# Cross attention's output projection inside its loop over pairs of heads, and the first loads of two stages in another order

## What is computed

```
x = x + cross_attention(layernorm(x), ctx)      # 16 heads of 128, keys: 8 x 256 rows of 256
x = x + linear_attention(layernorm(x))          # 16 heads of 128, gated
x = x + mixture_of_experts(layernorm(x))        # 32 experts, top 6, and 2 shared ones

q, k = rmsnorm(x @ Wq) * gq, rmsnorm(ctx @ Wk) * gk ;  v = ctx @ Wv     # cross attention
out  = softmax(q k^T / sqrt(128)) v             # per batch and head, 64 x 256 scores
return out.reshape(512, 2048) @ Wo              # the output projection: 16 heads summed
```

## Time and profile before

| | |
|---|---|
| median of 3 executions | 1117.15 us (1112.55 to 1118.06) |
| the profiled execution, its own time | 1118.14 us |
| its span, first to last instruction | 1116.2 us |
| mean granted TensorE clock | 0.971 |
| busy: PE, PEld, DVE, ACT, POOL | 90%, 74%, 58%, 48%, 24% |
| busy in tenths over the loop of pairs, 118.7 to 355.3 us | PE 8 to 9, DVE 5, ACT 6 |

### The profile page before, as it was taken

The page is one execution under the profiler, slowest core; times in us unless marked ns, Lnnn a source line. Parts: engine busy times, 40 slices in busy tenths (PEclk is TensorE's granted clock), DMA queues, the critical chain, the costliest instruction groups (busy, mean ns, idle before and its releaser), DMA issues.

```text
span 1116.2 us, 17886 instructions
## 1 busy us (share of the span) xinstructions
PE 1008.8 (90%) x5300; PEld 829.5 (74%) x5301; DVE 649.0 (58%) x947; ACT 540.2 (48%) x888; POOL 271.5 (24%) x188
## 2 busy tenths in 40 slices
PE   6999799999998869999999998798987988898982
PEld 5787589889987648888888876676865766666761
DVE  5655355555554567777777855564555656665663
ACT  5444466666664336555555434412444545453550
POOL 2200111111111442333333224100222322232221
PEclk9999999999999979999999999999999999999897
DMA  8000622222221621221221053104498989998996
GB/s 301 1 1 1 195 71 73 70 67 74 75 85 58 170 86 57 75 69 65 73 70 62 19 181 90 38 4 146 121 294 259 306 237 315 312 297 246 320 291 153
DMA packets 107145, 151.46 MB, mean 136 GB/s; under 512 B 11888, under 2 KB 73584, under 8 KB 106992
## 3 DMA queue, kind: packets, MB, share of 16 engines
q1 hardware_dynamic: 98816, 131.48, 37.6%
q0 software_dynamic: 8304, 19.67, 8.1%
HBM read 150.99 MB, written 14.55 MB: 148 GB/s over the span
## 4 chain that ended last, share of the span: by engine, by line
PE 62%; DMA 12%; issue 11%; DVE 5%; SPq 4%; ACT 3%; POOL 2%; POOLq 0%; DVEq 0%; ACTq 0%
PE ps L303 14%; PE ps L304 13%; PE ps L305 13%; DMA w_raw<-in_w 9%; PE ps L818 6%; PE ps L614 4%; PE ps L589 4%; POOL wo_l L402 2%; DVE w_l L830 1%; ACT w_h L825 1%; PE ps L568 1%; PE ps L673 1%; PE ps L601 1%; PE ps L680 1%; PE ps L690 1%
## 5 line engine op out<-in xcount | busy, mean ns | idle before, releaser
L830 DVE TENSOR_TENSOR w_l<-w_raw,w_h 128x1408 fp32r<-128x1408 f32 x78 | 127.2, 1647 | 72.6 <-ACT w_h L825 72.5
L825 ACT ACTIVATE w_h<-w_raw 128x1408 fp32r<-128x1408 f32 x78 | 106.0, 1375 | 105.4 <-DMA w_raw<-in_w 99.0
L818 PE MATMUL ps<-w_raw,hT 128*128 (+3 forms) x264 | 122.0, 598 | 8.2 <-DMA w_raw<-in_w 7.1
L303 PE MATMUL ps<-w_h,xeT_h 128*128 x288 | 101.5, 352 | 26.1 <-DVE w_l L830 25.8
L636 POOL TENSOR_TENSOR lw_l<-lw_raw,lw_h 128x1024 fp32r<-128x1024 f32 x32 | 76.5, 2395 | 148.4 <-ACT lw_h L632 147.9
L918 POOL DMA_INDIRECT xe<-xn_scratch,take x39 | 38.5, 987 | 282.5 <-DVE ob L891 198.7
L304 PE MATMUL ps<-w_l,xeT_h 128*128 x288 | 96.0, 333 | 0.0
L305 PE MATMUL ps<-w_h,xeT_l 128*128 x288 | 95.7, 332 | 0.0
L818 PEld LDWEIGHTS ps<-w_raw,hT 128*128 128x128 f32 (+1 forms) x264 | 48.0, 190 | 52.6 <-issue 51.6
L303 PEld LDWEIGHTS ps<-w_h,xeT_h 128*128 128x128 f32 x288 | 56.6, 197 | 35.6 <-issue 35.4
L303 PE MATMUL ps<-xT_hi,lw_h 128*128 128x512 f32 x192 | 77.2, 402 | 0.0
(11 more groups left out here) (285 smaller groups left out, 2516.7 us busy)
## 6 DMA issues: line engine op xcount, KB each, us to landing
w_raw<-in_w SPq DMA_DIRECT2D x82, 704.0 KB
w_raw<-in_w SPq DMA_DIRECT2D x40, 512.0 KB
rkB<-rk_scratch SPq DMA_DIRECT2D x64, 128.0 KB, 3.1
w_raw<-in_w SPq DMA_DIRECT2D x40, 192.0 KB
wq_raw<-in_Wq SPq DMA_DIRECT2D x8, 512.0 KB, 4.9
wo_raw<-in_Wo SPq DMA_DIRECT2D x16, 256.0 KB, 2.8
lw_raw<-in_kwT SPq DMA_DIRECT2D x8, 512.0 KB, 3.3
lw_raw<-in_qwT SPq DMA_DIRECT2D x8, 512.0 KB, 3.3
```

The source lines that it names most:

```text
L303: nc.tensor.matmul(out_ap, lh, rh, start=first, stop=False)
L818: m = e.matmul(ps[:, 6 + k, :], hT[r, k, c, :], part_of(w2_raw, w, r, c, every), start=c == 0, stop=c == FC - 1)
L825: e.activation(w13_h[:, k, :, f], w13_raw[:, k, :, f], ACT.Copy).then_inc(w13_hi_s, 1)
L830: e.tensor_tensor(w13_l[:, k, :, f], w13_raw[:, k, :, f], w13_h[:, k, :, f], ALU.subtract).then_inc(w13_ready, 1)
```

## The change

- In the pair loop a new set of helpers (`xo_*`) does the projection of pair i - 1 on TensorE in pair i, between scores and queries, into banks 2, 3, 6 and 7, and VectorE adds the four banks to x at once, so x takes eight partial sums instead of one. Heads are rounded straight from the accumulator; `aoT` is no longer used here. Pair 7's projection stands behind the loop. Pair 0 is written out of the loop.
- The waits of `xa_pe_ss` and of the first two `xa_pe_pT` now include the additions of the banks that they reuse.
- SyncE: pair 1's query and key weights are loaded before the scratch is written; `rkB` of pair 0 comes in 2 loads of 512 KB instead of 8 of 128 KB, ahead of the zeros, which now follow pair 1's loads; the projection's weights are loaded pair by pair in the loop.
- Linear attention's first loads are issued behind the last pair's loads, held by nothing; their buffers no longer share memory with cross attention's.
- `wo_*` keep only linear attention's use.

```diff
+        YB = (2, 3, 6, 7)
+        def xo_act_weights(e, i):
+            if not isinstance(i, int) or i > 0:
+                e.wait_ge(y_ps, i * TT)
+            for k in range(2):
+                e.wait_ge(wo_in[k], i * 16 + 16)
+                e.activation(wo_h[:, k, :], wo_raw[:, k, :], ACT.Copy).then_inc(wo_hi_s, 1)
+        def xo_pool_weights(e, i):
+            for k in range(2):
+                e.wait_ge(wo_hi_s, i * 2 + (k + 1))
+                e.tensor_tensor(wo_l[:, k, :], wo_raw[:, k, :], wo_h[:, k, :], ALU.subtract).then_inc(wo_ready, 1)
+        def xo_act_heads(e, i):
+            for k in range(2):
+                e.wait_ge(ao_ps, i * 2 + (k + 1))
+                e.activation(ao_h[:, k, :], ps[:, 6 + k, :], ACT.Copy).then_inc(ao_hi_s, 1)
+        def xo_dve_heads(e, i):
+            for k in range(2):
+                e.wait_ge(ao_hi_s, i * 2 + (k + 1))
+                e.tensor_tensor(ao_l[:, k, :], ps[:, 6 + k, :], ao_h[:, k, :], ALU.subtract).then_inc(ao_split, 1)
+        def xo_pe(e, i):
+            e.wait_ge(wo_ready, i * 2 + 2)
+            e.wait_ge(ao_split, i * 2 + 2)
+            for t in range(TT):
+                tk = slice(t * P, (t + 1) * P)
+                for k in range(2):
+                    m = mm3(ps[:, YB[t], :], ao_h[:, k, tk], ao_l[:, k, tk], wo_h[:, k, :], wo_l[:, k, :], k == 0, k == 1)
+                m.then_inc(y_ps, 1)
+        def xo_dve(e, i):
+            for t in range(TT):
+                e.wait_ge(y_ps, i * TT + (t + 1))
+                e.tensor_tensor(x[:, t, :], x[:, t, :], ps[:, YB[t], :], ALU.add).then_inc(x_ready, 1)
...
-        def xa_pe_ss(e, p):
+        def xa_pe_ss(e, p, added=None):
+            if added is not None:
+                e.wait_ge(x_ready, added * TT + 2)
...
-        def xa_pe_pT(e, i, j):
+        def xa_pe_pT(e, i, j, added=None):
+            if added is not None:
+                e.wait_ge(x_ready, added * TT + (j + 3))
...
+            pair_weights(1)
             e.wait_ge(rkT_ready, 2)
...
+            for k in range(2):
+                e.dma_start(rkB[k * SQ:(k + 1) * SQ, :, :].rearrange("p b n -> p (b n)"),
+                            rk_dram.ap()[k:k + 1, :].to_broadcast([SQ, NKV])).then_inc(rkB_first, 16)
...
+            pair_rest(1)
+            pair_weights(2)
+            pair_out(1)
...
+            with e.Fori(2, HP - 1) as p:
+                pair_rest(p)
+                pair_weights(p + 1)
+                pair_out(p)
+            pair_rest(HP - 1)
+            pair_out(HP - 1)
+            for n in range(4):
                 e.dma_start(lw_raw[n][:, :, :], lw_r[n][0]).then_inc(lw_in[n], 16)
...
                 xa_pool_wv(e, i)
+                xo_pool_weights(e, i)
...
                     xa_act_q(e, i + 1, 1)
+                xo_act_weights(e, i)
                 xa_act_pT(e, i, 0)
...
                     xa_act_qp(e, i + 1)
+                xo_act_heads(e, i)
...
                 xa_dve_norm(e, i, 3)
+                if y is not None:
+                    xo_dve(e, y)
...
-                xa_dve_ao(e, i)
+                xo_dve_heads(e, i)
+            pair(0, True)
+            with e.Fori(1, HP - 1) as i:
+                pair(i, True, i - 1)
+            pair(HP - 1, False, HP - 2)
+            e.wait_ge(ao_split, H)
+            e.sem_inc(ao_ready, H)
+            xo_dve(e, HP - 1)
...
-            def pair(i, more):
+            def pair(i, more, y=None):
                 for j in range(JB):
                     xa_pe_scores(e, i, j)
+                if y is not None:
+                    xo_pe(e, y)
...
-                else:
-                    wo_pe_first(e, 0)
+                xa_pe_pT(e, i, 0, y)
+                xa_pe_pT(e, i, 1, y)
...
+            xo_pe(e, HP - 1)
```

More of the change, by code:

```diff
@@ L100, in perceiver_block @@
         ao_l = sbuf(attn, "ao_l", [P, 2, T], F32R)
+        lw_raw = [sbuf(attn, f"lw_raw{n}", [P, DC, 2 * P]) for n in range(4)]
+        v_bias = sbuf(attn, "v_bias", [P, INNER])
+        ob_B = sbuf(attn, "ob_B", [P, D])
+        kq_b = sbuf(attn, "kq_b", [P, 2, H])
+        bw_raw = sbuf(attn, "bw_raw", [P, DC, H])
+        bb_B = sbuf(attn, "bb_B", [P, H])
         xat = ExitStack()
@@ L136, in perceiver_block @@
         lin = ExitStack()
+        aoT = sbuf(lin, "aoT", [P, H, T])
         xn_b = sbuf(lin, "xn_b", [P, TT, D])
-        lw_raw = [sbuf(lin, f"lw_raw{n}", [P, DC, 2 * P]) for n in range(4)]
         lw_h = [sbuf(lin, f"lw_h{n}", [P, DC, 2 * P], F32R) for n in range(4)]
@@ L402, in wo_pool_head, with wo_first, wo_act @@
             e.tensor_tensor(wo_l[:, k, :], wo_raw[:, k, :], wo_h[:, k, :], ALU.subtract).then_inc(wo_ready, 1)
-        def wo_first(e, n, head):
+        def wo_first(e, head):
             for k in range(2):
-                head(e, n, 0, k)
-        def wo_act(e, n):
-            for a, b, between in spans(n):
+                head(e, 0, k)
+        def wo_act(e):
+            for a, b, between in spans():
                 with e.Fori(a, b) as i:
                     for k in range(2):
-                        wo_act_head(e, n, i, k)
+                        wo_act_head(e, i, k)
@@ L550, in xa_dve_u @@
                             ALU.subtract).then_inc(u_ready, 1)
-        def xa_dve_ao(e, i):
-            for k in range(2):
-                e.wait_ge(ao_ps, i * 2 + (k + 1))
-                e.tensor_copy(aoT[:, bass.ds(i * 2 + k, 1), :], ps[:, 6 + k:7 + k, :]).then_inc(ao_ready, 1)
         def xa_pe_q(e, p, k):
@@ L1019, in _ @@
                             zeros[:, :].unsqueeze(1).to_broadcast([P, TT + 1, D])).then_inc(scratch_io, 16)
-            rk_r = rk_dram.ap().rearrange("(h k) (j n) -> h k j n", k=2, j=JB)
-            def rk_load(p, j):
-                for k in range(2):
-                    src = rk_r[bass.ds(p, 1), k, j, :]
-                    e.dma_start(rkB[k * SQ:(k + 1) * SQ, 2 * j:2 * j + 2, :].rearrange("p b n -> p (b n)"),
-                                src.to_broadcast([SQ, 2 * SKV])).then_inc(rkB_in[j], 16)
@@ L1029, in _ @@
-            for j in range(JB):
-                rk_load(0, j)
-            with e.Fori(1, HP) as p:
-                e.wait_ge(wq_ready, p)
-                e.dma_start(wq_raw[:, :, :], wq_r[bass.ds(p, 1)].rearrange("h p c n -> p (h c) n")).then_inc(wq_in, 16)
-                e.wait_ge(wkT_ready, p)
-                e.dma_start(wkT_raw[:, :, :], wkT_r[bass.ds(p, 1)].rearrange("h p k c -> p (h k) c")).then_inc(wkT_in, 16)
-                e.wait_ge(wv_ready, p)
-                e.dma_start(wv_raw[:, :, :], wv_r[bass.ds(p, 1)].rearrange("h p c n -> p (h c) n")).then_inc(wv_in, 16)
-                for j in range(JB):
-                    e.wait_ge(s_ready, p * 4 + (j - 3))
-                    rk_load(p, j)
@@ L1614, in pair @@
                 xa_pe_ao(e, i)
-            with e.Fori(0, HP - 1) as i:
-                pair(i, True)
-            pair(HP - 1, False)
-            wo_pe(e, 0)
+            pair(0, True)
+            with e.Fori(1, HP - 1) as i:
+                pair(i, True, i - 1)
+            pair(HP - 1, False, HP - 2)
+            xo_pe(e, HP - 1)
+            e.wait_ge(y_ps, X1)
+            e.sem_inc(wo_mm, H)
             layernorm_pe(e, 1, xn_b)
```

176 lines of the change are left out of this document (91 added, 85 removed).

## The result

The changed kernel takes 1097.74 us (median of 4, 1094.45 to 1099.91), the kernel before beside it 1115.09: ratio 0.9841, 95% interval 0.9808 to 0.9874, 17.4 us less. It lies 6.3 us under the forecast of 1104.0: 4.2 because the gain was larger, and 2.1 because the kernel before, taken at the 1117.15 of its three first executions, came out at 1115.09 beside it. The profiled execution took 1098.05 (span 1096.3, granted clock 0.971, as before).

What follows compares the result with a forecast made beforehand. TensorE was taken to bound the pair loop, 28.69 us a pair, with holes at both ends. Gains 9.4 + 2.5 + 1.2 = 13.1 took the profiled 1118.14 to 1105.0; the median lies 1.0 lower: 1104.0, range 1100 to 1111.

Steps and rivals of the forecast that it cites:

- Part 1: SyncE's first loads: the waits for `rkB` and split weights go, pair 0 takes 28.69 instead of 38.16; 9.4 us gained.
- Part 2: Projection moved into the pair loop: 45.55 - 33.6 - 0.6 - 1.75 - 7.1 = 2.5 us gained.
- Last pair's wait: Last pair's first transpose waits for VectorE's third sum, 14.1 into the pair instead of 12.34: 1.75 us lost.
- behind the loop: After the pair loop: pair 7's projection, 5.6, and the chain ahead of it, 1.50, stay: 7.1 us.
- I take 0.1 a pair: ScalarE's two extra weight roundings, 1.04 against a cover of 1.0 on TensorE: 0.1 us a pair, 0.6 in all.
- Part 3: Linear attention's first loads land during the last pair; the chain before didn't wait for them, so worth nothing by itself.
- The tail: Layer norm behind the projection: earlier GpSimd splits release the held output up to 1.9 us earlier; 1.2 taken.
- the 388.8 that was named: Sign to look for after the change: the projection's last product ends near 388.8 us.
- `rkB` late: Rival at the loop's start: `rkB` lands at 124.7 as before, the 3.1 us hole stays; 1107.1, chance 0.10.
- A wait in each pair: Rival in the loop: TensorE waits every pair, for instance with ScalarE's 1.04 us uncovered; 1110.7, chance 0.11.
- Tail unchanged and half of the start: Rival: no tail gain, another load's wait halves the start's gain; 1109.9, or 1113 with another loop wait; chance 0.04.
- GpSimd's new splits hold VectorE so that TensorE waits: Slower rival in the loop: two projection-weight splits of 1.2 us in each of seven pairs, 16.6 us; 1120.6, chance 0.03.

Runs made afterwards that it cites:

- p1_only: Kernel before with SyncE's new first-load order, each pair's query and key weights a pair earlier, pair 0 written out of the loops: 1102.53 us, ratio 0.9899.
- act_order: Changed kernel, but ScalarE rounds the projection's weights at a pair's end, ahead of the heads (last pair: behind the first two transposes): 1093.15 us, ratio 0.9823.
- after_lw_late: Changed kernel with SyncE's loads of linear attention held until all heads are ready, as in the kernel before: 1116.81 us, ratio 1.0029.
- pool_late: Changed kernel with GpSimd's splits for linear attention held until half of the last projection is done: 1102.38 us, ratio 0.9873.
- both: As act_order, and in the last pair the projection of the pair before goes to banks 2, 3, 0 and 1: 1094.98 us, ratio 0.9844.

## Why the prediction was right and wrong

- **Part 1, 9.4.** Right: 9.1 to 9.9 by stage; pair 0 took 29.0 in *p1_only* and 29.3 in the changed kernel, instead of 38.0. Its margin was luck. I took `v_bias` for the duration, with landing 2.0 before use; it was 0.2. The two loads landed 5.0 and 7.3 after the first issue. The Trainium skill's rule that two loads of 64 partitions each run one behind the other (SBUF — State Buffer, "Can I just issue two DMAs to hit both halves?") gives by that estimate 7.4 us from the first issue, at 110.7: landed at 118.1. The trace agrees to 0.1: 118.0.
- **Part 2, 2.5.** Right in sign, under half in size: 1.0 by stage. In the profiled execution, from the first score of pair 1 on, it is 1.4 (45.55 - 35.25 - 1.71 - 7.19, with 207.41 - 172.16 = 35.25 and 28.12 - 26.41 = 1.71), and pair 0 loses 0.3 of that. Last pair's wait 1.71 (1.75 in the sum), behind the loop 7.19 (7.1), both right. The term that was off is ScalarE's: "I take 0.1 a pair" was 0.30 to 0.39, and with pair 0 and its own roundings 2 to 2.7 in all instead of 0.6, as *act_order* shows by taking it away. The cover of 1.0 for 1.04 left no room for the time between a releaser and its waiter.
- **Part 3, "worth nothing by itself".** No run has it alone on the kernel before. Beside Part 2 it isn't so: without it the changed kernel loses all it gained (*after_lw_late*). The sum isn't touched by it, but the reason was wrong: that the chain before didn't wait for these loads held only as long as the projection ran behind the loop, and Part 2 removes that.
- **The tail, 1.2.** Mis-sized: 2.8. The shorter hold, for which the 1.2 stood, gave 1.4, nearly right. The other 1.4 is the beta product, put at nothing because it "keeps its idle gap ahead and its clock". It doesn't always: it took 3.6 with full clock in two of the four executions of the changed kernel, 5.0 in the two others, and never under 5.4 in the kernel before. *pool_late*, with the counts given there, shows that both hang on the splits' start, the beta product with a chance of its own on top. That GpSimd and VectorE's tensor-scalar operation can exclude each other for a whole instruction is what the Trainium skill says (SBUF — State Buffer, Who interferes with whom), and the runs agree: 897 and 2569 ns by GpSimd's start alone, each ending 0.28 behind GpSimd.
- **The step that failed is the sum's frame.** It set every stage that isn't edited to nothing, and "the range: below" named only products, beta and tail. These stages gave 4.9. And it took the profiled execution less 1.0, from three executions 5.5 apart, for the kernel before: its median was 2.1 lower in the comparison, and 1113.8 to 1115.0 in the three sets of 15 to 18 executions. I read the spread as that of the median and not as that of single waits which each execution, and perhaps a moved program, can win or lose.
- **What was luck.** That the edited stages gave 13.4 for 13.1: Part 2 fell short by 1.5 and the tail gave 1.6 more. That the last product ended at 388.2, near the 388.8 that was named: the keys' stage ended 2.5 earlier in that execution, and without that it would have been 390.7.
- **The rivals.** `rkB` late: no. A wait in each pair: it was there, at 0.30 to 0.39 of the 1.04. Tail unchanged and half of the start: no. GpSimd's new splits hold VectorE so that TensorE waits: no, TensorE is busy for 206.64 of 207.41.

*act_order* and *both* are the best versions run: in cross attention 2.7 and 4.2 us under the changed kernel, by their totals not yet told from it.

## What to carry to other kernels

When work moves off the end of a stage, ask what it covered there: loads that "nobody waited for" are waited for next, and here that alone was 17 us. A cover that equals to 0.1 us what it has to hide is a wait, not a cover. And a range must hold what stages far from the edit do from one execution to the next: here they differed by up to 6.6 us between executions of the kernel before, in part by holes of 2 to 3 us behind which the clock falls or not. Take the median of the kernel before from more than three executions, too.

## What was not expected of the hardware

The same program with the same 2.64 us hole at 41 us had a granted clock of 1.00 behind it in one execution and 0.52 in another. One load of a small table in pieces of 4 bytes (`kq_b`) held SyncE for 6.38 us in *after_lw_late* and 8.03 in the changed kernel, as the last of ten loads in a row, and for 1.81 in the kernel before; in the first two it landed 9.1 to 10.6 us after its issue.
